# Five f32 projections of a fused layer written as three f16 products each

## What is computed

```python
xn = layernorm(x)
q = xn @ Wq
latent = (xn @ Wk + xn @ Wv) @ W_down_kv
k, v = latent @ W_up_k, latent @ W_up_v
scores = (q_head @ k_head.T) / 16 * exp(-1e-4 * abs(i - j))
x = x + layernorm(softmax(scores) @ v_head @ Wo)
x = x + layernorm(quantized(layernorm(x) @ H) @ ternary(weight).T)
```

## Time and profile before

| what | value |
|---|---|
| median of 3 executions | 1438.04 us (1435.0 to 1438.44) |
| span of the profiled execution, first to last instruction | 1433.2 us; its own device time is not given apart |
| mean granted TensorE clock | 0.983 |
| busy share of the span | PE 94%, PEld 42%, DVE 82%, ACT 77%, POOL 58% |
| f32 projections on TensorE: q, k, v, lat | 126.8, 45.0, 34.8, 34.7 us busy |

### The profile page before, as it was taken

One profiled execution on the slowest core, in us unless ns is written; L12 is line 12 of the kernel. 1 busy time (PEld: TensorE's weight loads), 2 busy tenths in 40 slices (PEclk: granted clock), 3 DMA queues, 4 the chain that ended last, 5 costly groups with the idle time before them and its releaser, 6 DMA issues.

```text
span 1433.2 us, 35971 instructions
## 1 busy us (share of the span) xinstructions
PE 1349.5 (94%) x12330; PEld 600.5 (42%) x12330; DVE 1179.9 (82%) x2739; ACT 1098.2 (77%) x1125; POOL 834.7 (58%) x1238
## 2 busy tenths in 40 slices
PE   5889999999999999999999999999999999999863
PEld 3334444444444444444444444444444444443332
DVE  7567888888888888888888888888888888888655
ACT  1878787888888788878878887887888787787831
POOL 4223655666565666556557655656765655675446
PEclk9999999999999999999999999999999999999986
DMA  6455456556555645656564565655556555555420
GB/s 194 154 167 170 154 172 202 155 164 206 164 182 173 197 156 166 206 157 190 173 190 157 173 201 157 193 175 187 156 177 194 163 185 184 176 156 175 128 77 31
DMA packets 174557, 241.45 MB, mean 168 GB/s; under 512 B 28336, under 2 KB 145200, under 8 KB 174512
## 3 DMA queue, kind: packets, MB, share of 16 engines
q1 hardware_dynamic: 140176, 206.78, 46.5%
q10 hardware_dynamic: 34336, 34.08, 7.7%
HBM read 154.80 MB, written 69.21 MB: 156 GB/s over the span
## 4 chain that ended last, share of the span: by engine, by line
PE 76%; DVE 8%; issue 5%; ACT 4%; DMA 3%; SPq 2%; POOL 2%; DVEq 0%; ACTq 0%; POOLq 0%
PE heads_ps L720 27%; PE scores_ps L707 16%; PE misc_ps L603 8%; PE misc_ps L635 7%; PE misc_ps L660 4%; PE misc_ps L614 3%; PE misc_ps L587 3%; ACT probs L909 2%; DVE x_hl L1204 2%; PE misc_ps L595 2%; PE misc_ps L678 2%; DVE diagonal L1253 2%; DVE weighted L1161 2%; PE misc_ps L625 2%; PE misc_ps L669 1%
## 5 line engine op out<-in xcount | busy, mean ns | idle before, releaser
L909 ACT ACTIVATE probs<-scores_ps 128x1024 f32<-128x1024 f32 x768 | 759.8, 1026 | 248.0 <-PE scores_ps L707 247.9
L720 PE MATMUL heads_ps<-probs,v_sb 128*32 128x512 f32 x4096 | 525.4, 603 | 3.6 <-DVE heads L1150 1.9
L1253 DVE TENSOR_TENSOR diagonal<-scores_ps,comp 128x1024 f32<-128x1024 f32 x256 | 312.2, 1219 | 70.1 <-PE scores_ps L707 70.1
L707 PE MATMUL scores_ps<-q_rep,k_rep 64*128 64x128 f16 (+2 forms) x5120 | 324.6, 251 | 16.0 <-DVE diagonal L1253 9.2
L707 PEld LDWEIGHTS scores_ps<-q_rep,k_rep 64*128 64x128 f16 x5120 | 165.6, 94 | 348.7 <-DVE diagonal L1253 149.5
L916 ACT ACTIVATE probs<-diagonal 128x2048 f32<-128x2048 f32 x128 | 246.0, 1922 | 0.0
L996 POOL TENSOR_TENSOR ln_neg_mean<-zero,ln_moments 128x4 f32<-128x4 f32 (+1 forms) x131 | 34.6, 264 | 356.5 <-DVE ln_moments L1115 356.3
L1161 DVE SCALAR_TENSOR_TENSOR weighted<-misc_ps,edges 128x384 f32<-128x384 f32 x256 | 129.4, 547 | 64.3 <-PE misc_ps L603 33.8
L720 PEld LDWEIGHTS heads_ps<-probs,v_sb 128*32 128x32 f32 x4096 | 91.5, 108 | 171.7 <-issue 169.8
L1038 POOL TENSOR_TENSOR q_hl<-weighted,q_hl 128x768 f16<-128x768 f32 x64 | 105.5, 1648 | 77.5 <-DVE q_hl L1168 77.5
L1043 POOL TENSOR_TENSOR heads_c<-heads_c,den_spread 128x1024 f32<-128x1024 f32 (+1 forms) x33 | 75.7, 2296 | 111.0 <-DMA den_spread<-den_scratch 111.0
(11 more groups left out here) (132 smaller groups left out, 1511.5 us busy)
## 6 DMA issues: line engine op xcount, KB each, us to landing
q_rep<-q_scratch SPq DMA_DIRECT2D x128, 384.0 KB, 4.3
k_rep<-k_scratch SPq DMA_DIRECT2D x256, 192.0 KB, 3.9
q_scratch<-q_hl SPq DMA_DIRECT2D x64, 384.0 KB, 2.6
k_scratch<-k_hl SPq DMA_DIRECT2D x64, 384.0 KB, 3.1
x_in<-in_L_attn_x_dram ACTq DMA_DIRECT2D x32, 512.0 KB, 4.9
heads_c<-heads SPq DMA_DIRECT2D x256, 64.0 KB, 2.5
x_res<-in_L_attn_x_dram ACTq DMA_DIRECT2D x32, 512.0 KB, 6.8
den_spread<-den_scratch SPq DMA_DIRECT2D x256, 64.0 KB, 2.3
```

The source lines that it names most:

```text
L707: ins = mm(scores_ps[:, place + par, at:at + n * P], k_rep[rows, pair, kv_, k_cols], q_rep[rows, pair, qv_, q_cols], start=True, stop=True)
L720: ins = mm(heads_ps[W32 * g:W32 * (g + 1), :], v_sb[:, b.slot, kt, at:at + W32], probs[:, quad % 2, g, kt, :], start=(kt == 0), stop=(kt = ...
L909: nc.scalar.activation(flat[:, :, at:at + S], scores_ps[:, place:place + 2, :], ACT.Exp, scale=EXP_SCALE).then_inc(off_probs, 1)
L1253: v.tensor_tensor(diagonal[:, quad % 2, 2 * two:2 * two + 2, :], scores_ps[:, place:place + 2, :], comp[:].rearrange("p t n -> p (t n)").u ...
```

## The change

The weights of the five projections and their two moving operands are kept as f16 high and low halves, and each f32 product becomes three f16 products: high times high, high times low, low times high. The weights are scaled by 1024 before they are split, and the factors are taken out where VectorE weights q and k and where it takes v. ScalarE now takes the high half of xT and lat out of PSUM, and VectorE makes the low half as the difference, where it copied before. The opening splits the weights; `path_choice` has one more bound. The rest of the diff writes each stage's group into the step tables instead of a dictionary (`pv_end` and `heads_end` become `pv` and `heads` with group "a"), keeps the f32 weights in a buffer that the loop uses later, and moves one wait into `compact`; the tables' order of the stages that were there does not change. Cut to its core:

```diff
+W_GAIN = 2.0 ** 10
+WEIGHT_BOUND = 32.0
 SCALAR_STEPS = {
-    4: [("load_res", 0)], 12: [("x1T", 0)], 14: [("x1T", 1)], 15: [("load_x", 0)], 21: [("round_x", 0)],
+    4: [("load_res", 0, "a"), ("xT", 0, "pre")], 6: [("xT", 1, "pre")], 9: [("lat", 0, "pre")], 12: [("x1T", 0, "b")], 14: [("x1T", 1, "b")],
...
+PRODUCTS = ((0, 0), (0, 1), (1, 0))
...
             def lat_stage(b, part, piece):
...
+                    for c in range(DC):
+                        for n, (wh, xh) in enumerate(PRODUCTS):
+                            for half in range(2):
+                                ins = mm(misc_ps[LAT * half:LAT * (half + 1), bank, 0:S // 2], w_lat_hl[:, wh, c, :],
+                                         xT_hl[:, xh, c, half * S // 2:(half + 1) * S // 2], start=(c == 0 and n == 0),
+                                         stop=(c == DC - 1 and n == len(PRODUCTS) - 1))
...
             def q_stage(b, part, piece):
...
+                    for n, (wh, xh) in enumerate(PRODUCTS):
+                        ins = mm(misc_ps[:, BANK["q", part], :], wq_hl[:, wh, piece, part * P:(part + 1) * P], xT_hl[:, xh, piece, :],
+                                 start=(piece == 0 and n == 0), stop=(piece == DC - 1 and n == len(PRODUCTS) - 1))
...
+            def x_high_take(b, part):
+                act.wait_ge(in_psum["xT"], part_count("xT", b, part))
+                nc.scalar.activation(xT_hl[:, 0, part, :], misc_ps[:, BANK["xT", part], :], ACT.Copy).then_inc(x_high, 1)
+
+            def lat_high_take(b, part):
+                act.wait_ge(in_psum["lat"], part_count("lat", b, 0))
+                nc.scalar.activation(latT_hl[:, 0, :], misc_ps[:, BANK["lat", part], 0:S // 2], ACT.Copy).then_inc(lat_high, 1)
...
             def xT_take(b, part):
...
-                v.tensor_copy(xT[:, part, :], misc_ps[:, BANK["xT", part], :]).then_inc(taken["xT"], 1)
+                bank = misc_ps[:, BANK["xT", part], :]
...
+                dve.wait_ge(x_high, part_count("xT", b, part))
+                v.tensor_tensor(xT_hl[:, 1, part, :], bank, xT_hl[:, 0, part, :], ALU.subtract).then_inc(taken["xT"], 1)
```

More of the change, by code:

```diff
@@ L61 @@
 DISTANCE_OF = {"load": 2, "pre": 1, "own": 0, "a": -1, "b": -2, "c": -3}
[L62 to L70, removed]
@@ L87 @@
 }
 VECTOR_STEPS = {
[L89 to L93, removed]
-}
@@ L95 @@
[L95 to L98, removed]
+    1: [("z", 0, "c"), ("z", 1, "c"), ("x1_make", "b")], 2: [("xT", 0, "pre")],
@@ L137, in bank_table @@
     table, age = {}, [0, 0, 0]
-    for n, (stage, part, _) in enumerate(ORDER_ALL, 1):
+    for n, (stage, part, _, _) in enumerate(ORDER_ALL, 1):
         if (stage, part) in table:
@@ L471, in compact @@
                 sp.wait_ge(heads_done, opened + count(HQ, b, 2 * (half + 1)))
+                if half == 0 and b.buffers == 2 and not (isinstance(b.number, int) and b.number == 0):
+                    sp.wait_ge(in_psum["y"], part_count("y", b.other(-1), 1))
                 for g in range(4):
@@ L736, in iteration @@
                         scores(b, h, not post_a)
-                    for stage, part, piece in TENSOR_STEPS.get(h, []):
-                        if present[GROUP[stage]]:
-                            stages[stage](b.other(DISTANCE[stage]), part, piece)
+                    for stage, part, piece, group in TENSOR_STEPS.get(h, []):
+                        if present[group]:
+                            stages[stage](b.other(DISTANCE_OF[group]), part, piece)
             def enter_loop(loop, b):
@@ L745, in enter_loop @@
                     await_taken(*held)
-                for stage, part, _ in ORDER_ALL:
-                    before = b.other(DISTANCE[stage] - 1)
+                for stage, part, _, group in ORDER_ALL:
+                    before = b.other(DISTANCE_OF[group] - 1)
                     holder[BANK[stage, part]] = (stage, part, before)
@@ L782, in weight_norms @@
                                  start=(ci == 0), stop=(ci == DC - 1))
+                pe.wait_ge(w_squared, 1)
+                mm(scores_ps[:, 3, D:2 * D], ones, sq_up[:, 0, :], start=True, stop=False)
+                for ci in range(DC):
+                    mm(scores_ps[:, 3, D:D + LAT], ones, sq_lat[:, ci, :], start=False, stop=False)
+                ins = mm(scores_ps[:, 3, D:2 * D], ones, sq_up[:, 1, :], start=False, stop=True)
                 ins.then_inc(setup_pe, 1)
@@ L806, in opening_batch @@
                 turn_ternary()
+                pe.wait_ge(w_low, 1)
                 k_stage(b, 0, 0)
@@ L825, in general_path @@
                 for stage, parts in PARTS.items():
-                    if GROUP[stage] == "pre":
+                    if stage in PRE:
                         pe.wait_ge(taken[stage], parts)
@@ L831, in general_path @@
                     holder[:] = [None] * CLOSING_BANKS
-                    for stage, part, piece in GENERAL_ORDER["before"]:
+                    for stage, part, piece, _ in GENERAL_ORDER["before"]:
                         stages[stage](b, part, piece)
@@ L856, in general_path @@
                             ins.then_inc(g_pv, 1)
-                    for stage, part, piece in GENERAL_ORDER["after"]:
+                    for stage, part, piece, _ in GENERAL_ORDER["after"]:
                         stages[stage](b, part, piece)
@@ L921, in iteration @@
                 for h in range(STEPS):
-                    for stage, part in SCALAR_STEPS.get(h, []):
-                        if present[GROUP[stage]]:
-                            takes[stage](b.other(DISTANCE[stage]), part)
+                    for stage, part, group in SCALAR_STEPS.get(h, []):
+                        if present[group]:
+                            takes[stage](b.other(DISTANCE_OF[group]), part)
                     if own and h % 4:
@@ L1261, in iteration @@
                         weigh_diagonal(b, h // 4, not post_a)
-                    for step, *part in VECTOR_STEPS.get(h, []):
-                        if present[GROUP[step]]:
-                            steps[step](b.other(DISTANCE[step]), *part)
+                    for step, *part, group in VECTOR_STEPS.get(h, []):
+                        if present[group]:
+                            steps[step](b.other(DISTANCE_OF[group]), *part)
             def ternary_weights():
```

181 lines of the change are left out of this document (130 added, 51 removed), and 15 rows, old and new, of tables (TENSOR_CLOSING, TENSOR_STEPS).

## The result

The changed kernel takes **1532.81 us** (1530.31 to 1535.18, four runs) against 1437.83 us for the kernel before on the same chip: a ratio of 1.067, 95% interval 1.065 to 1.069. The forecast was 1441.4, its range ended at 1456.

A forecast was written before the change was run, and what follows sets the result against it. TensorE's queue order was taken as the bound: 1.16 us lost by step 11 less 1.06 won back, 0.10 per batch, 3.0 over 30 batches, plus 0.4 for the opening, on 1438.04 gives 1441.4 us; range 1424 to 1456.

The forecast's parts named there:

- The rest lies beside other work: Remaining work of the loop: v's changed take and ScalarE's 1.6 us more per batch fill idle time, costing nothing.
- What TensorE saves: TensorE's q, latent, v and k stages: f16 products save 1.96 us per batch, 1.8 at the least.
- The price of the products: TensorE's f16 stages: q part 1.40 us instead of 1.91, latent and v 0.75 instead of 1.01, k part 0.43.
- the prediction's own rule: TensorE stage cost: time scales with streamed columns, apart from some 0.12 us for the change from stage to stage.
- The chain in front: Copy, low half, diagonal, scores: step 6 loses 1.05 us, and TensorE is 1.16 later by step 11.
- the walk: Step-by-step timing of one iteration in the old timeline's clock: step 11's scores start at 631.07, 1.16 us later.
- the rival that priced it at 571: ScalarE's copy of lat costs 571 ns like L888, delaying step 11's scores: 1447.1 us, slower; chance 0.18.
- What is won back behind it: Steps 15, 17 and 23 behind step 11: 1.19 us saved, 0.13 of it lost, so 1.06 per batch.
- The opening: Before the loop: four more products and a wider check add 0.4 us (0 to 1.5).
- The first rival: ScalarE's first copy of xT is not held up, the chain to step 11 0.47 us earlier: 1427.7 us; chance 0.17.
- The second rival: TensorE's saving of 1.96 us per batch arrives whole, 58.8 us less: 1379.6 us; chance 0.05.

The follow-up runs named there:

- the version with 60 instructions: Changed kernel plus 60 waits on a semaphore passed long before, ahead of the opening's v products, where TensorE's sequencer waits: 1453.18 us.
- ScalarE's order changed alone: Changed kernel with the 60 added instructions, and ScalarE's first copy of x moved ahead of issuing the residual's load: 1441.81 us.
- the best version: Changed kernel with 60 added instructions, ScalarE's first x copy ahead of the load's issue, VectorE's low halves behind step 4's diagonal and ahead of x1's statistics: 1417.41 us.

## Why the prediction was wrong

**The step that failed is "The rest lies beside other work".** It put at nothing, without a reason, what TensorE spends on getting its own instructions. "What TensorE saves" had priced the new products by columns, 1.96 us per batch, and never counted them as instructions, though 64 more per pass stood in the change. The view that would have raised the question is the page's part on DMA queues: 27 packets of q8 for a program whose loop runs 13 times means that the loop is not loaded again, and 1666 instructions are 6.5 packets. No rival of the four was near it. In the profiled runs the loads account for 1532.0 - 1451.7 = 80.3 us of span: TensorE's listed waits grew by 54.3 (182.8 less 128.5) and its busy time, at the lower clock (0.954 against 0.980), by 26.8 (1334.8 less 1308.0).

- **The price of the products was right.** q 623.36 - 621.96 = 1.40 (1.40 forecast), the latent 0.77 (0.75 forecast, 0.765 by the prediction's own rule), from the timeline after. As groups, the four f32 forms went from 241.3 us busy to 181.6.
- **The chain in front was right, to 0.1 us.** Step 6's scores come 618.74 - 610.76 = 7.98 us behind step 0, before 6.86: 1.12 lost, 1.05 forecast. The latent 9.88 against 8.44: 1.44 (1.38). Step 11's scores start 13.39 behind step 0, by the walk 631.07 - 617.73 = 13.34; the stage behind them 1.26 later than before (1.16). ScalarE's copies are these, in groups by form:

```profile
L924 ACT ACTIVATE xT_hl<-misc_ps 128x512 f16<-128x512 f32 x64 | 38.3, 599 | 9.1 <-issue 7.7 <-PE misc_ps L606 1.3
L928 ACT ACTIVATE latT_hl<-misc_ps 128x256 f16<-128x256 f32 x32 | 12.3, 385 | 2.7 <-PE misc_ps L621 2.7
```

  The copy of lat takes 385 ns, estimated at 0.38, so the rival that priced it at 571 falls. The Trainium skill, "ScalarE: Activation LUTs", section "What ACT_TABLE_LOAD costs", gave an estimated 399 ns for it; the trace's 385 is close to that.
- **"What is won back behind it" was too much.** Forecast 1.06 of 1.16 per batch. In the version with 60 instructions an undisturbed iteration takes some 42.14 us, 0.31 over the 41.83 of the earlier trace rows, so 0.94 of the 1.25 lost by step 11 there came back. And eight of the 25 periods in the middle took 42.85 to 43.17: in the one I read, step 26's scores waited 0.81 us for a second diagonal, which VectorE made behind a long cast of q (last section). Over all 31 periods that makes 15.2 us (1313.5 against 1298.3) instead of 3.0. The opening is a smaller miss: the first diagonal product comes at 36.4 us instead of 34.4, 2.0 late where 0.4 was forecast.
- **The first rival** (the first copy not held up: 1427.7; its own terms add up to 1427.3) described a better kernel, not this one. With ScalarE's order changed alone it gives 1441.81, 11 us less than 1453.18 where the rival had 14; to get clearly under the kernel before it took VectorE's order as well.
- **The second rival** (the saving arrives whole: 1379.6) stayed far off: the best version takes 1417.41, since VectorE's diagonal comes last there instead.

## What to carry to other kernels

Count a loop's instructions per engine, not only its columns, and read the instruction queue: if its packets do not grow with the passes, the loop stays loaded, and an edit of a few per cent more instructions, or of code ahead of it, can end that; here it cost 80 us, over four times what the edit itself took (15 us) or, in a better order, gave (19). Before judging such an edit, shift the loop by several amounts and look again (here 60 and 91 instructions helped, 29 did not). A copy that is split over two engines belongs behind an instruction that a third engine waits for, if its own result is needed later.

## What the runs showed of the hardware

- **Instruction loading.** In these runs a TensorE loop that spans up to seven packets of 256 instructions is loaded once, a longer one is loaded over and over (nearly nine packets per pass), and TensorE stops near the start of the pass. The Trainium skill, "Runtime: NRT & Kernel Launch", section "Instruction fetch mechanics", gives TensorE 2048 instructions, refilled in blocks of 256, calls the cost of crossing a block mostly hidden, and says that a taken branch to a target outside the current window of two pages (blocks) has to wait until the target is fetched. The blocks agree with the packets, and the first stop, right behind the loop's branch, agrees with the wait; the second lies at the next packet bound and is not hidden. Together they are 52.9 us in 12 passes, and 80 with what follows. But a loop that spans seven packets takes the same 12 branches without one packet, so two pages are too few for TensorE in these runs. That seven, not eight, stay fits every run here; why was not tried.
- **VectorE's cast of q beside GpSimd.** VectorE casts q twice per batch. In the version with 60 instructions the first cast takes 0.56 us in every batch, the second, beside GpSimd's work, 0.56 to 2.04. In the iteration with the second wait the second cast started 0.16 us behind GpSimd's low half of k and took 1.91, and the diagonal behind it came late (GpSimd's timeline, VectorE's, then TensorE's):

```profile
746.72 1.65 POOL L1107 TENSOR_TENSOR k_hl<-weighted,k_hl 128x768 f16<-128x768 f32 x1
```

```profile
746.88 1.91 DVE L1259 CAST q_hl<-weighted 128x768 f16<-128x768 f32 x1
748.71 1.21 DVE L1344 TENSOR_TENSOR diagonal<-scores_ps,comp 128x1024 f32<-128x1024 f32 x1
```

```profile
749.98 0.61 PE L750 MATMUL scores_ps<-q_rep,k_rep 64*128 64x256 f16 x8 [0.81 <-DVE diagonal L1344]
```

  In an undisturbed one it started 0.10 ahead, and GpSimd's took 1.98 instead of 1.65 (VectorE's timeline, then GpSimd's):

```profile
620.28 0.56 DVE L1259 CAST q_hl<-weighted 128x768 f16<-128x768 f32 x1
```

```profile
620.38 1.98 POOL L1107 TENSOR_TENSOR k_hl<-weighted,k_hl 128x768 f16<-128x768 f32 x1
```

  Who starts second waits. The Trainium skill, "SBUF — State Buffer", section "Who interferes with whom", states just this of casts and GpSimd; the trace agrees. The eight long periods are exactly those whose second cast took 1.40 to 2.04 us; in the other 17 it took 0.56 to 0.94, and the period 42.12 to 42.44. Above the usual 42.16 the eight hold some 7 of the 15.2 us. The kernel before has long casts too, up to 1.48 us in its 25 periods, of which none is over 42.32; with both orders changed the second cast took at most 1.02 in these periods, and none of them is over 41.35. No run changed the cast alone, so that it is the cause in all eight rests on the one chain shown.
